# Turning the attention weights by a transposing DMA instead of TensorE, with the start and the end of the attention stage rearranged

## The chip, the cores and the metric

The kernel runs on one core of one Trainium2 chip. The metric is the device time of one execution in microseconds (us); the median of three executions stands below. Everything after that section comes from one profiled execution.

## What is computed

Four layers are applied to `x` (64 sequences of 64 tokens, 512 channels, float32), each added to its input; `c` is a condition vector for each sequence.

```python
def attention(x, c):                       # 16 heads of 32 channels
    scale, shift = split(c @ W_emb + b_emb)
    xn = rms_norm(x, g_norm) * (1 + scale) + shift
    q, k, v = heads(xn @ W_qkv)
    P = softmax(rms_norm(q, g_q) @ rms_norm(k, g_k).T * 32 ** -0.5)
    o = P @ v
    return o + o @ W_out
x = x + attention(x, c)
x = x + sample(x, c)       # each channel becomes w0 * x[i0] + w1 * x[i0 + 1]
x = x + gru(c, x)          # h0 = c; 64 steps with W_ih, W_hh
x = x + oscillators(c, x)  # q0 = p0 = c; 64 steps of Runge-Kutta 4, four tanh(q) @ coupling.T in a step
```

## The kernel before

Each matrix product is made of float16 halves (a high part and a rest, so three products for one), accumulated in float32. A "low" operation computes the rest of a value whose high part has been rounded.

**Stage one** (to about 640 us) does attention and sampling on 32 pairs of sequences, 128 tokens on the 128 partitions. It is a software pipeline written out by hand: slot `i` of each engine holds pieces of five pairs. On TensorE (PE) the order of a slot is: `turn_qk` (q and k of pair i-1), `project(i, 0)`, `scores(i-1)`, `turn_p(i-2)`, `project(i, 1)`, `mix(i-2)` (P @ v), `project(i, 2)`, `proj(i-2)`, `sample(i-3)`, `turn_x(i+2)`. Every engine runs its own list in order and waits on semaphores. After the slots, the last pairs (N3, N2, N1, N0, with N0 the very last) are written out one by one.

The part around the change is the path of P. `scores` leaves the logits in PSUM (`psB`); `least` (VectorE, DVE) takes minima; `exps` (ScalarE, ACT) writes `S`, 16 activations a pair, the last 14 at the end of the slot; `invert_sum` (DVE) and `norm_p` (GpSimd, POOL) normalize `S` (128 x 1024 float32). In the next slot `turn_p` makes eight float32 transposes of 128 x 128 into `psA`, `high_p` (ACT) and `low_p` (DVE) copy them, in two parts, into the float16 halves of `PT`, and `mix` reads `PT`.

Sampling of pair p: the sync engine's queue (SP) loads row numbers (`load_rows`), DVE builds one-hot matrices `E` (`build`), `high_x1` and `low_x1` (ACT, POOL) split the attention result, `move_x1` copies it one row further by three SBUF-to-SBUF transfers (tap 1), `sample` multiplies both taps by `E`, `weigh_taps` (DVE) and `add_taps` (POOL, two operations for a sequence) add the result to `XR`. ACT's line L483 is one helper for all its operations, so its rows are told apart by the tiles.

In the same stage, weights for the second stage are converted piece by piece (`load_wr`, `high_wr`, `low_wr`, `store_wih`), with stage buffers in `room`.

**Stage two** (from about 644 us) is 64 steps of both recurrences. `first()` begins with `high_xs(0)` (ACT), which waits for all taps of all pairs, then `low_xs(0)` (POOL), then on PE `gi_front(0)` and the other gate products of step 0, `stage(0, 0)` (the first coupling product of the oscillators, which needs only the condition), then `gi_front(1)`. There is one buffer `xs`: `high_xs(1)` waits until the gate products of step 0 have read it.

Of the kernel before, what the change touches and what calls it, by code (L numbers as in the profile page):

```python
# [5 lines left out]
ALU = mybir.AluOpType  # L6
# [55 lines left out]
def program(nc, x, cond, W_emb, b_emb, g_norm, W_qkv, g_q, g_k, W_out, W_ih, W_hh, b_ih, b_hh,  # L62
# [9 lines left out]
    with ExitStack() as ctx:  # L72
# [22 lines left out]
        x2_done = sem("x2_done")  # L95
        first4 = sb("first4", [PART, 4, KC, B])
        block = ctx.enter_context(nc.Block())
        with ExitStack() as s:
            attention_and_sampling(nc, ctx, s, block, banks, S, x2_done, first4, XR, condT, ident, Wx, later, x, cond, W_emb, b_emb, g_norm,
                                   W_qkv, g_q, g_k, W_out, W_ih, W_hh, b_ih, b_hh, coupling, bias, rows_dram, wih_dram)  # L100
        with ExitStack() as s:
            recurrences(nc, ctx, s, block, banks, S, x2_done, first4, XR, condT, later, out)


def attention_and_sampling(nc, sems, ctx, block, banks, S_, x2_done, first4, XR, condT, ident, Wx, later, x, cond, W_emb, b_emb, g_norm,
# [37 lines left out]
    split = [front[:, 2 + u, :].bitcast(F16).rearrange("p (i n) -> p i n", i=2) for u in range(2)]  # L143
# [7 lines left out]
    hs0 = first4[:, 0, :, :].rearrange("p c b -> p (c b)").bitcast(F16).rearrange("p (i c b) -> p i c b", i=2, c=KC)  # L151
    S = sb("S", [PART, HEADS, T])
# [12 lines left out]
    stage = [room[k % 2][:, (2 + k // 2) * D:(3 + k // 2) * D] for k in range(4)]  # L165
# [18 lines left out]
    Elast = [room[u][:, KC * D // 2:].bitcast(F16).rearrange("p (c n) -> p c n", c=KC) for u in range(2)]  # L184
    psE = psQ[:, 0, :].rearrange("p (m b) -> p m b", m=2 * KC)
    xT = psB[:, 0, :].rearrange("p (c b t) -> p c b t", c=KC, b=2)
    rsT = psB[:, 1, 0:PART]

# [24 lines left out]
    cond_T, cond_kept, w1_T, emb_done, mod_step = (sem(n) for n in ("cond_T", "cond_kept", "w1_T", "emb_done", "mod_step"))  # L213
    wq_hi, wq_ready, wq_scaled, brz_done = (sem(n) for n in ("wq_hi", "wq_ready", "wq_scaled", "brz_done"))
    wv_hi, wv_ready, mod_ready, wo_scaled, gain_step = (sem(n) for n in ("wv_hi", "wv_ready", "mod_ready", "wo_scaled", "gain_step"))
    x_in = [sem(f"x_in{u}") for u in range(2)]
    rows_in = [sem(f"rows_in{u}") for u in range(2)]
    last_blank, x1_moved, last_moved = sem("last_blank"), sem("x1_moved"), sem("last_moved")
# [16 lines left out]
    wr_in = [sem(f"wr_in{k}") for k in range(4)]  # L235
# [38 lines left out]
    def _(sp):  # L274
# [46 lines left out]
        def slot(pair, i):  # L321
            if p := pair(3):
                load_x(p)
# [13 lines left out]
            if 0 <= i + 2 - WR_FROM < WR_PIECES:  # L337
                load_wr(i + 2 - WR_FROM)
# [8 lines left out]
        for k in range(3 * KC):  # L347
            if k == 0:
                load_x(FIRST2[0])
            if k == 0:  # L350
                for at, g in ((10 * KC, g_q), (10 * KC + 1, g_k)):
                    sp.dma_start(vrows[at:at + 1, :].rearrange("a (q n) -> a q n", n=DH),
                                 g.rearrange("(a q n) -> a q n", a=1, q=1).broadcast_to([1, PART // DH, DH])).then_inc(rows_of_v_in, 16)
# [17 lines left out]
    def _(pool):  # L371
# [30 lines left out]
        def add_taps(p, b):  # L402
            pool.wait_ge(um_done, p.n * 2 + b + 1)
            us = um[b][:, :, 0, :]
            nc.gpsimd.tensor_tensor(us, us, um[b][:, :, 1, :], ALU.add).then_inc(us_done, 1)
            pool.wait_ge(us_done, p.n * 2 + b + 1)
            r = of_b(p, b)
# [31 lines left out]
        def slot(pair, i):  # L439
# [1373 lines left out]
```

## Time and profile before

| | |
|---|---|
| three runs | 1569.5, 1569.72, 1570.03 us; median 1569.72 |
| the profiled execution | 1567.16 us |
| its span (first to last instruction) | 1565.3 us |
| PE busy | 1511.4 us, 97% |
| DVE busy | 1360.1 us, 87% |
| ACT busy | 943.3 us, 60% |
| POOL busy | 688.2 us, 44% |

The span is cut into instructions of each engine, with the time an engine sat idle before one in square brackets and what ended the wait. A "line" is the line of the source. A timeline row merges instructions that follow each other: its first number is when the first began, its second how long they took. PE's own lengths are modelled: a row ends a little after the next one begins, so the time of a group is read from one start to the next.

### The profile page before, as it was taken

The numbers are of one execution on the slowest core, as the hardware profiler recorded it, in microseconds if no ns is written. First come the engines' busy times: TensorE is split into PE (matmuls) and PEld (weight loads), VectorE is DVE, ScalarE is ACT, GpSimd is POOL, SyncE is SP. The second block draws the span as 40 slices with busy tenths as digits, with TensorE's granted clock in tenths as the row PEclk, the third lists the DMA queues.
The fourth block names the chain that finished last, engine by engine and source line by source line (L and its number), as shares of the span: only waits on it lengthen the run. The fifth ranks groups of instructions, "written<-read, shape, count | busy, mean of one in ns | idle before, by whom it ended". The sixth has DMA issues, their size and how long they took to land.

```text
span 1565.3 us, 95993 instructions
## 1 busy us (share of the span) xinstructions
PE 1511.4 (97%) x42395; PEld 1347.4 (86%) x42395; DVE 1360.1 (87%) x3317; ACT 943.3 (60%) x2884; POOL 688.2 (44%) x853
## 2 busy tenths in 40 slices
PE   5999999999999999899999999999999999999994
PEld 3577777777777777899999999999999999999994
DVE  7988888888888888589989899989998999899997
ACT  6677776777777764355555555555555555555553
POOL 2455555555555554434343434334343434334331
PEclk8999999999999999999999999999999999999998
DMA  6112221222222213000000000000000000000001
GB/s 226 40 58 58 63 58 56 62 65 70 73 70 77 63 33 111 23 11 15 13 14 15 15 14 12 16 15 14 13 13 15 15 14 12 15 15 15 13 13 16
DMA packets 106658, 59.87 MB, mean 38 GB/s; under 512 B 77369, under 2 KB 91873, under 8 KB 106241
## 3 DMA queue, kind: packets, MB, share of 16 engines
q1 hardware_dynamic: 106160, 53.71, 13.2%
q8 instruction: 333, 5.46, 1.5%
q14 instruction: 85, 0.69, 0.1%
q10 hardware_dynamic: 80, 0.02, 0.0%
HBM read 33.71 MB, written 11.60 MB: 29 GB/s over the span
## 4 chain that ended last, share of the span: by engine, by line
PE 92%; DVE 3%; issue 2%; ACT 0%; DMA 0%; SPq 0%; POOL 0%; POOLq 0%; DVEq 0%; ACTq 0%
PE psB L1390 34%; PE psA L1419 15%; PE psQ L1108 14%; PE psA L1424 7%; PE psQ L1149 7%; PE psO L1179 5%; PE psO L1167 2%; PE psA L1117 2%; PE psB L1131 2%; PE psA L1086 2%; PE psB L1188 1%; DMA vrows<-in_L_cond_g_k 0%; DVE Wx L837 0%; DVE room L751 0%; PE psQ L1204 0%
## 5 line engine op out<-in xcount | busy, mean ns | idle before, releaser
L1390 PE MATMUL psB<-first,Wx 128*128 128x64 f16 x9216 | 290.9, 193 | 3.3 <-issue 2.4
L1419 PE MATMUL psA<-ts,Cp 128*128 128x64 f16 x8192 | 283.0, 193 | 11.1 <-ACT ts L1458 10.8
L1390 PE MATMUL psB<-first,Whh 128*128 128x64 f16 x9072 | 286.4, 193 | 0.7
L1390 PEld LDWEIGHTS psB<-first,Wx 128*128 128x128 f16 x9216 | 278.2, 98 | 4.2 <-issue 3.9
L1390 PEld LDWEIGHTS psB<-first,Whh 128*128 128x128 f16 x9072 | 273.7, 98 | 1.5 <-issue 1.4
L1108 PE MATMUL psQ<-Wx,front 128*128 128x512 f16 x1152 | 267.4, 382 | 4.6 <-DVE front L914 3.9
L1458 ACT ACTIVATE ts<-qst 128x256 f16<-128x256 f32 x192 | 80.1, 417 | 314.5 <-DVE qst L1561 314.5
L1419 PEld LDWEIGHTS psA<-ts,Cp 128*128 128x128 f16 x8192 | 258.0, 98 | 12.5 <-ACT ts L1458 11.7
L1108 PEld LDWEIGHTS psQ<-Wx,front 128*128 128x128 f16 x1152 | 110.7, 98 | 122.3 <-DVE front L914 4.1
L1424 PE MATMUL psA<-ts,Cp 128*128 128x64 f16 x4096 | 162.4, 193 | 0.0
L1699 POOL TENSOR_TENSOR en<-rz,dn 128x256 f32<-128x256 f32 x64 | 46.7, 729 | 256.6 <-issue 255.8
L1424 PEld LDWEIGHTS psA<-ts,Cp 128*128 128x128 f16 x4096 | 137.9, 98 | 0.0
L412 POOL TENSOR_TENSOR S<-S,rden 128x1024 f32<-128x1024 f32 x32 | 60.9, 1904 | 172.0 <-DVE rden L813 172.0
L1588 DVE TENSOR_TENSOR ts<-psA,ts 128x256 f16<-128x256 f32 x256 | 107.7, 421 | 31.5 <-ACT psA L1458 26.1
L483 ACT ACTIVATE S<-psB,mn 128x64 f32<-128x64 f32 x448 | 132.9, 337 | 1.6 <-DVE mn L797 1.6
L751 DVE TENSOR_SCALAR room<-rows,lidx 128x512 f16<-128x512 f16 x256 | 126.9, 538 | 0.0
L1561 DVE SCALAR_TENSOR_TENSOR rest<-cub,psQ 128x256 f32<-128x256 f32 x256 | 106.6, 416 | 6.9
L1149 PE MATMUL psQ<-x,room 128*128 128x128 f16 x1856 | 108.5, 219 | 0.0
L1561 DVE SCALAR_TENSOR_TENSOR psO<-qst,psO 128x256 f32<-128x256 f32 x256 | 106.6, 416 | 0.0
L1699 POOL TENSOR_TENSOR V<-X3b,first 128x256 f32<-128x256 f32 x64 | 46.8, 731 | 136.0 <-DVE first L1683 135.9
L1149 PEld LDWEIGHTS psQ<-x,room 128*128 128x128 f16 x1856 | 104.9, 98 | 0.1
L483 ACT ACTIVATION_READ_ACCUMULATOR S<-psB,mn 128x1 f32 x448 | 103.5, 231 | 0.0
(192 smaller groups left out, 3021.6 us busy)
## 6 DMA issues: line engine op xcount, KB each, us to landing
front<-in_x SPq DMA_DIRECT2D x32, 256.0 KB, 2.6
rows<-rows_dram SPq DMA_DIRECT2D x64, 128.0 KB, 2.9
out<-ot SPq DMA_DIRECT2D x512, 16.0 KB, 1.8
x<-x SPq DMA_DIRECT2D x29, 224.0 KB
Whh<-in_L_cond_W_qkv SPq DMA_DIRECT2D x12, 256.0 KB, 6.7
room<-in_L_cond_W_hh SPq DMA_DIRECT2D x12, 256.0 KB, 3.0
room<-in_L_cond_W_ih SPq DMA_DIRECT2D x12, 256.0 KB, 2.8
wih_dram<-front SPq DMA_DIRECT2D x12, 256.0 KB, 3.0
```

The lines of the kernel that those rows point to most:

```text
L483: return nc.scalar.activation(out, in_, f, **k)
L751: e = v.tensor_scalar(E_of(p, b)[:, k, :], rows[b][:, :], lidx[:, k:k + 1], None, ALU.is_equal)
L1108: last = mm(psQ[:, n, :], xn[p.u][:, i, c, :], Wqkv[:, j, c, n * D:(n + 1) * D], start=(c == 0 and t == 0), stop=(c == KC - 1 and t == 2))
L1149: last = mm(o[:, m, :, :], E_of(p, b)[:, c, m * PART:(m + 1) * PART], x1_of(p)[:, :, i, c, b, :], start=(c == 0 and i == 0), stop=(c == KC ...
L1179: last = mm(psO[:, m, :], Wo[:, i, c, m * PART:(m + 1) * PART], oT[:, j, c, :], start=(c == 0 and t == 0), stop=(c == KC - 1 and t == 2))
L1390: last = mm(o, W_[:, i, c, g * PART:(g + 1) * PART], src[:, j, c, :], start=False, stop=False, skip_group_check=True)
L1419: mm(psF[:, s % 2, m, :], Cp[:, i, c, m * PART:(m + 1) * PART], ts_[:, 0, c, :], start=(c == 0 and m == 0 and i == 0), stop=False, skip_gr ...
L1424: last = mm(psF[:, s % 2, m, :], Cp[:, 0, c, m * PART:(m + 1) * PART], ts_[:, 1, c, :], start=False, stop=(c == KC - 1), skip_group_check= ...
L1458: return nc.scalar.activation(out, in_, f, **k)
L1561: return v.scalar_tensor_tensor(out=flat(out), in0=flat(in0), scalar=scalar, in1=flat(in1), op0=ALU.mult, op1=op1)
L1588: v.tensor_tensor(ts_[:, 1, :, :], th, ts_[:, 0, :, :], ALU.subtract).then_inc(S["ts_ready"], 1)
L1699: return nc.gpsimd.tensor_tensor(flat(out), flat(in0), flat(in1), op)
```

## The change

For pairs 0 to 29 (N2) P is no longer turned by PE. ACT's `high_halves` and POOL's `low_halves` split `S` as it lies (128 x 1024) into `halves`, and SP's `turn_p` sends one transposing DMA of 128 x 2048 float16 (512 KB) from `halves` into `PT`. `mix` waits for that transfer. N1 and N0 are still turned by PE. To make room, `load_wr` has two stage buffers, not four, and `split` lies in `room`.

At the start, `g_q` and `g_k` are loaded from ACT's queue and not SP's; `low_wq` of two pieces stands ahead of the slots, and `grid_middle` (two casts on DVE) in slot 1 and not ahead of slot 0; `modulation` stands behind `newton` and one `low_wq`.

At the end, the last pair is sampled in two parts: tap 0 (which needs no moved copy) and then tap 1; `weigh_last_taps` and `first_taps` do the first two time steps on their own, so that `high_xs(0)` waits only for these. The oscillators' first coupling product stands in stage one behind the last sample.

```diff
@@ sync engine
+        def turn_p(p):
+            sp.wait_ge(pl_done, p.n + 1)
+            need(sp, mix_done, p.n)
+            sp.dma_start_transpose(PT[:, :, :, :].rearrange("p i j n -> p (i j) n"), halves.rearrange("p i s k -> p (i s k)"))\
+                .then_inc(pt_in, 16)
...
         def slot(pair, i):
+            if p := pair(-2):
+                turn_p(p)
             if p := pair(3):
                 load_x(p)
...
-            if k == 0:
-                for at, g in ((10 * KC, g_q), (10 * KC + 1, g_k)):
-                    sp.dma_start(vrows[at:at + 1, :].rearrange("a (q n) -> a q n", n=DH),
@@ GpSimd
+        def first_taps(p, b):
+            pool.wait_ge(um_first, b + 1)
+            us = um[b][:, :, 0, 0:FIRST_T]
+            nc.gpsimd.tensor_tensor(us, us, um[b][:, :, 1, 0:FIRST_T], ALU.add).then_inc(us_first, 1)
+            pool.wait_ge(us_first, b + 1)
+            r = of_b(p, b)[:, :, 0:FIRST_T]
+            nc.gpsimd.tensor_tensor(r, r, us, ALU.add).then_inc(x2_first, 1)
...
+        def low_halves(p):
+            pool.wait_ge(ph_done, p.n + 1)
+            nc.gpsimd.tensor_tensor(halves[:, 1, :, :], S[:, :, :], halves[:, 0, :, :], ALU.subtract).then_inc(pl_done, 1)
...
             if p := pair(-1):
                 norm_p(p)
+                if p.n <= N2.n:
+                    low_halves(p)
@@ ScalarE
+        def high_halves(p):
+            act.wait_ge(p_done, p.n + 1)
+            need(act, pt_in, p.n * 16)
+            a(halves[:, 0, :, :], S[:, :, :]).then_inc(ph_done, 1)
...
-            if p := pair(-2):
-                high_p(p, 0)
-                high_p(p, 1)
...
             if 0 <= i - WR_FROM < WR_PIECES:
                 high_wr(i - WR_FROM)
+            if p := pair(-1):
+                high_halves(p)
...
-        high_p(N2, 1)
-        high_v(N0)
         high_o(N2)
         high_qk(N0, 0)
         high_qk(N0, 1)
+        high_v(N0)
...
         high_o(N0)
+        a(Q0, condT[:, :, :]).then_inc(S_["Q_done"], 1)
+        act.wait_ge(S_["Q_done"], 1)
+        a(ts_[:, 0, :, :], Q0, ACT.Tanh).then_inc(S_["ts_hi"], 1)
+        a(th0, Q0, ACT.Tanh).then_inc(S_["th_done"], 1)
         high_x1(N0)
@@ VectorE
-            if p := pair(-2):
-                low_p(p, 0)
-                low_p(p, 1)
...
+        for k in range(2 * KC + 2, 3 * KC):
+            low_wq(k)
-        grid_middle()
...
-        build(N1, 1, (0, 1, 2))
+        build(N1, 1, range(KC))
         residual(N0)
-        build(N1, 1, (3,))
...
-        weigh_taps(N0, 0)
-        weigh_taps(N0, 1)
+        dve.wait_ge(S_["th_done"], 1)
+        v.tensor_tensor(ts_[:, 1, :, :], th0, ts_[:, 0, :, :], ALU.subtract).then_inc(S_["ts_ready"], 1)
+        weigh_last_taps(0)
+        weigh_last_taps(1)
@@ TensorE
             if b == 0:
-                pe.wait_ge(pt_ready, p.n + 1)
+                if p.n <= N2.n:
+                    pe.wait_ge(pt_in, 16 * (p.n + 1))
+                else:
+                    pe.wait_ge(pt_ready, p.n - N2.n)
...
-            if p := pair(-2):
-                turn_p(p)
...
-        sample(N0, 0)
-        sample(N0, 1)
+        sample_last(0, 0)
         cell_from_condition(2)
+        sample_last(1, 0)
+        sample_last(0, 1)
+        sample_last(1, 1)
+        oscillators_from_condition()
@@ stage two
             if n == 0:
+                act.wait_ge(x2_done, B - 2)
+                act.wait_ge(x2_first, 2)
+            if n == 2:
                 act.wait_ge(x2_done, B)
...
-            stage(Pair(0, 0, 0), 0)
             gi_front(1)
```

PE, one middle slot before, from `turn_qk` to `sample`:

```order
L1086 MATMUL psA<-ident,qn 128x128 x8
L1108 MATMUL psQ<-Wx,front 128x512 x12
L1131 MATMUL psB<-first 64x64 x96
L1117 MATMUL psA<-ident,S 128x128 x8
L1108 MATMUL psQ<-Wx,front 128x512 x12
L1167 MATMUL psO<-PT,Vt 32x64 x96
L1108 MATMUL psQ<-Wx,front 128x512 x12
L1179 MATMUL psO<-oT,Wo 128x128 x48
L1149 MATMUL psQ<-x,room 128x128 x64
```

and the same slot after:

```order
L1141 MATMUL psA<-ident,qn 128x128 x8
L1163 MATMUL psQ<-Wx,front 128x512 x12
L1187 MATMUL psB<-first 64x64 x96
L1163 MATMUL psQ<-Wx,front 128x512 x12
L1241 MATMUL psO<-PT,Vt 32x64 x96
L1163 MATMUL psQ<-Wx,front 128x512 x12
L1253 MATMUL psO<-oT,Wo 128x128 x48
L1205 MATMUL psQ<-x,room 128x128 x64
```

The row `psA<-ident,S` is gone; in the new slot `mix` (`psO<-PT,Vt`) follows `project(i, 1)` as before, with eight transposes less ahead of it.

POOL, the end of one middle slot and the next, after:

```order
L432 TENSOR_TENSOR S<-S,rden 128x1024
L437 TENSOR_TENSOR front<-S,front 128x1024
L453 TENSOR_TENSOR front<-front,modA 128x512
L453 TENSOR_TENSOR front<-front,modB 128x512
L425 TENSOR_TENSOR um<-um 128x4x64
L428 TENSOR_TENSOR XR<-XR,um 128x4x64
L425 TENSOR_TENSOR um<-um 128x4x64
L428 TENSOR_TENSOR XR<-XR,um 128x4x64
L447 TENSOR_TENSOR x<-XR,x 128x4x64 x2
L460 TENSOR_TENSOR front<-front 128x512
```

The row `front<-S` is `low_halves` (`halves` lies in the tensor `front`). It stands between `norm_p` and the next slot's `modulate` (`modA`, `modB`), ahead of the adding of taps (`um`) and of `low_x1` (`x<-XR,x`); before the change nothing stood there.

SP, one middle slot after:

```order
L317 DMA_TRANSPOSE PT<-front 128x16x128
L285 DMA front<-in_x 128x512
L289 DMA rows<-rows_dram 128x512
L302 DMA x<-x 112x1024
L302 DMA x<-x 15x1024
L304 DMA x<-x 1x2x384
L312 DMA room<-in_L_cond_W_ih 128x512
L323 DMA wih_dram<-room 256x1x512
L289 DMA rows<-rows_dram 128x512
```

The transposing DMA is the first row of the slot; all others are as before and wait behind it.

PE, the last pair and the first step of the recurrences, before:

```order
L1149 MATMUL psQ<-front,room 128x128 x64
L1225 MATMUL psB<-first,Whh 128x64 x48
L1149 MATMUL psQ<-qn,room 128x128 x64
L1225 MATMUL psB<-first,Whh 128x64 x48
L1380 UNCONDITIONAL_BRANCH
L1390 MATMUL psB<-first,Wx 128x64 x144
L1419 MATMUL psA<-ts,Cp 128x64 x32
L1424 MATMUL psA<-ts,Cp 128x64 x16
L1390 MATMUL psB<-first,Wx 128x64 x144
```

and after:

```order
L1205 MATMUL psQ<-front,room 128x128 x64
L1299 MATMUL psB<-first,Whh 128x64 x48
L1219 MATMUL psQ<-qn,room 128x64 x32
L1299 MATMUL psB<-first,Whh 128x64 x48
L1219 MATMUL psQ<-qn,room 128x64 x96
L1308 MATMUL psA<-ts,Cp 128x64 x48
L1462 UNCONDITIONAL_BRANCH
L1472 MATMUL psB<-first,Wx 128x64 x288
L1472 MATMUL psB<-first,Whh 128x64 x144
```

The sample of N0 (`psQ<-qn,room`) is in two parts, with the last gate products from the condition (`first,Whh`) between; the coupling product (`psA<-ts,Cp`) has moved from between the gate products of steps 0 and 1 (`psB<-first,Wx`, 144 each) to ahead of both.

## Rows read from the trace of the kernel before

**Rows 1.** Windows: length, busy PE, PEld, DVE, ACT, POOL; clock, DMA share, GB/s.

```profile
66.00:586.80 520.80, 517.02 (x10077) 380.72 (x10074) 445.27 (x845) 376.43 (x1422) 279.76 (x278) 1.00 0.21 62
```

**Rows 2.** Timeline of PE, one slot: start us, us, engine, line, operation, count.

```profile
310.90 1.04 PE L1086 MATMUL psA<-ident,qn 128*128 128x128 f32 x8
...
315.36 1.09 PE L1117 MATMUL psA<-ident,S 128*128 128x128 f32 x8
...
316.29 2.75 PE L1108 MATMUL psQ<-Wx,front 128*128 128x512 f16 x12
...
318.97 1.20 PE L1167 MATMUL psO<-PT,Vt 64*32 64x64 f16 x96
...
325.38 3.74 PE L1149 MATMUL psQ<-x,room 128*128 128x128 f16 x64
...
329.51 1.04 PE L1086 MATMUL psA<-ident,qn 128*128 128x128 f32 x8
```

**Rows 3.** Source line L1190, the last transpose of a slot.

```profile
L1190 PE MATMUL psB<-ident,rs x32: 272/273/323, 17.3 to 571.3; 128*128 128x128 f32 x32
```

**Rows 4.** Timeline of DVE, ACT and POOL in the same slot.

```profile
317.12 1.29 DVE L790 TENSOR_TENSOR PT<-psA,PT 128x512 f16<-128x512 f32 x2
...
319.08 0.60 ACT L483 ACTIVATE front<-psQ 128x512 f32<-128x512 f32 x1 [0.99 <-PE psQ L1108]
...
325.40 0.25 DVE L813 RECIPROCAL rden<-den 128x16 f32<-128x16 f32 x1 [1.16 <-ACT S L483]
...
325.73 1.90 POOL L412 TENSOR_TENSOR S<-S,rden 128x1024 f32<-128x1024 f32 x1 [5.07 <-DVE rden L813]
...
312.18 1.09 POOL L429 TENSOR_TENSOR front<-front,modA 128x512 f32<-128x512 f32 x1 [3.02 <-DVE front L738]
...
317.93 1.61 POOL L423 TENSOR_TENSOR x<-XR,x 128x256 f16<-128x256 f32 x2
```

**Rows 5.** Groups by form, POOL, 82 to 585; timeline, ACT.

```profile
L436 POOL TENSOR_TENSOR front<-front 128x512 f16<-128x512 f32 x27 | 31.4, 1164 | 0.0
...
604.47 1.06 ACT L483 ACTIVATE S<-S 128x1024 f32<-128x1024 f32 x1 [0.81 <-DVE S L802]
```

**Rows 6.** Source L318 (512 KB loads); page, part 6; queues, 700 to 1500.

```profile
DMA to landing us min/median/max: 4.2/5.8/8.4
...
out<-ot SPq DMA_DIRECT2D x512, 16.0 KB, 1.8
...
q1 hardware_dynamic: 65154, 7.44, 6.4%
```

**Rows 7.** Timeline of the start.

```profile
11.57 0.33 PE L1270 MATMUL psO<-ident,vrows 42*128 42x42 f32 x1 [2.79 <-DMA vrows<-in_L_cond_g_k]
...
12.38 2.35 DVE L842 SCALAR_TENSOR_TENSOR room<-Wo,room 128x1024 f16<-128x1024 f32 x2
...
25.57 1.38 DVE L866 CAST x<-um 64x512 int32<-64x512 f32 x1
...
39.14 0.75 DVE L730 SCALAR_TENSOR_TENSOR first<-psA,gqk,first 128x512 f16<-128x512 f32 x1 [1.59 <-ACT first L483]
```

**Rows 8.** Timeline of the last pairs and of the first recurrence step.

```profile
601.49 0.60 ACT L483 ACTIVATE Vt<-psQ 128x512 f16<-128x512 f32 x1 [2.20 <-PE psO L1167]
...
633.06 1.47 SPq L294 DMA_DIRECT2D qn<-qn  x2
...
635.39 2.31 DVE L751 TENSOR_SCALAR room<-rows,lidx 128x512 f16<-128x512 f16 x4
...
637.22 3.73 PE L1149 MATMUL psQ<-qn,room 128*128 128x128 f16 x64 [2.55 <-issue]
...
643.49 0.42 ACT L1458 ACTIVATE first<-XR 128x256 f16<-128x256 f32 x1 [9.33 <-POOL XR L408]
...
644.76 4.54 PE L1390 MATMUL psB<-first,Wx 128*128 128x64 f16 x144 [2.41 <-issue]
...
649.34 0.42 ACT L1458 ACTIVATE first<-XR 128x256 f16<-128x256 f32 x1 [0.35 <-PE psB L1390]
```

More of the change, by code:

```diff
@@ L142, in attention_and_sampling @@
     rsB = sb("rsB", [PART, PART])
-    split = [front[:, 2 + u, :].bitcast(F16).rearrange("p (i n) -> p i n", i=2) for u in range(2)]
+    halves = front[:, 2:4, :].rearrange("p v n -> p (v n)").bitcast(F16).rearrange("p (i s k) -> p i s k", i=2, k=T)
     xa = front[:, 4, :].rearrange("p (c b t) -> p c b t", c=KC, b=2)
@@ L164, in attention_and_sampling @@
     wo32, cp32 = (r.rearrange("p (c n) -> p c n", c=KC) for r in room)
-    stage = [room[k % 2][:, (2 + k // 2) * D:(3 + k // 2) * D] for k in range(4)]
+    stage, split32 = ([room[v][:, (2 + k) * D:(3 + k) * D] for k in range(2)] for v in range(2))
+    split = [a.bitcast(F16).rearrange("p (i n) -> p i n", i=2) for a in split32]
     x1_last = [a.rearrange("p v n -> p (v n)").bitcast(F16).rearrange("p (v i c b t) -> p v i c b t", v=2, i=2, c=KC, b=2)
@@ L184, in attention_and_sampling @@
     Elast = [room[u][:, KC * D // 2:].bitcast(F16).rearrange("p (c n) -> p c n", c=KC) for u in range(2)]
+    psF0, th0 = (psA[:, n, 0:KC * B].rearrange("p (c b) -> p c b", c=KC) for n in range(2))
     psE = psQ[:, 0, :].rearrange("p (m b) -> p m b", m=2 * KC)
@@ L187, in attention_and_sampling @@
     rsT = psB[:, 1, 0:PART]
+    FIRST_T = 2
     def x1_of(p):
@@ L745, in build @@
                     need(dve, samp_done, p.n * 2 + b - 1)
+                elif b == 1:
+                    for u in range(2):
+                        dve.wait_ge(wih_out[u], 3 * KC // 2 * 16)
                 if p.n == 0:
@@ L1082, in turn_qk @@
             pe.wait_ge(qn_done, p.n * 2 + 2)
-            need(pe, pt_ready, p.n - 1)
+            need(pe, qk_ready, p.n)
+            if p.n == 0:
+                pe.wait_ge(cond_kept, 1)
             for n in range(2):
@@ L1151, in sample, with sample_last @@
             last.then_inc(samp_done, 1)
+        def sample_last(b, tap):
+            if tap:
+                pe.wait_ge(last_moved, 96)
+            else:
+                pe.wait_ge(x1_ready, NP)
+                pe.wait_ge(e_built, N0.n * 2 + b + 1)
+                pe.wait_ge(um_done, N0.n * 2 + b - 1)
+            for m in range(KC):
+                for c in range(KC):
+                    for i in range(2):
+                        last = mm(psL[b][:, m, tap, :], E_of(N0, b)[:, c, m * PART:(m + 1) * PART], x1_of(N0)[:, tap, i, c, b, :],
+                                  start=(c == 0 and i == 0), stop=(c == KC - 1 and i == 1))
+            if tap:
+                last.then_inc(samp_done, 1)
         def mix(p, b):
@@ L1227, in cell_from_condition, with oscillators_from_condition @@
                 last.then_inc(S_["gn_done"], 1)
+        def oscillators_from_condition():
+            for i, j in TERMS:
+                pe.wait_ge(S_["ts_ready"] if j else S_["ts_hi"], 1)
+                for c in range(KC):
+                    for m in range(KC):
+                        last = mm(psF0[:, m, :], Cp[:, i, c, m * PART:(m + 1) * PART], ts_[:, j, c, :],
+                                  start=(c == 0 and m == 0 and (i, j) == (0, 0)), stop=(c == KC - 1 and i == 1), skip_group_check=True)
+            last.then_inc(S_["f_done"], 1)
         def slot(pair, i):
```

152 lines of the change are left out of this document (83 added, 69 removed).

## The prediction

> **What bounds the kernel now.** I read the windows first, stage by stage. In slots 3 to 29 PE is busy 517.0 of 520.8 us (99.3%) at the full granted clock, level 2.4 GHz; DVE has 86%, ACT 72%, POOL 54% [rows 1]. So these slots cost what PE's list costs, and another engine matters only where it makes PE wait. The timeline of PE gives one slot: from `turn_qk` at 310.90 to the next at 329.51 is 18.61 us; the eight transposes of P take from 315.36 to 316.29, 0.93 us; `mix` begins at 318.97, 8.07 us into the slot; `sample` at 325.38 [rows 2]. The last transpose of a slot runs 32 times, the last at 571.3 [rows 3]. The reader should see two things there: no gap between PE's groups, and the place of `mix`, because that is where the new path ends. Outside these slots PE waits: at the start on loads and on DVE's conversions, at the end on chains through all engines and a DMA [rows 7, 8].
>
> **Middle slots: what goes.** PE loses 0.93 us a slot. For PE-bound slots that is the gain, if nothing new is waited for: slots 3 to 30 and the tail's transposes of N2, 29 times, 27.0 us. DVE also loses its two copies (1.29 us [rows 4]) and ACT its own; neither is the bound, so I count nothing.
>
> **Middle slots: the new chain.** Its end must come before `mix`. From rows 4: `norm_p` starts at 325.73 and takes 1.90, so P is ready at 327.63, 1.88 us before the next slot begins. All of this follows PE's `project(i, 1)` (ACT's square of it is at 319.08), which itself comes 0.93 earlier, so the distance to the next slot stays 1.88. Then `high_halves`: 1024 columns on ACT from SBUF to SBUF, as the exponential of S, 1.06 us [rows 5]; at that place ACT is idle, its row of `Vt` and one weight piece being done by about 326.4. `low_halves` on POOL: between the 1.90 of `norm_p`, with the same columns, and twice the 1.164 of a 512-column difference to f16, 2.33 [rows 4, 5]. With 0.05 between steps the transfer can be issued 1.2 to 1.6 us into the next slot; I take 1.3. `mix` comes 8.07 - 0.93 = 7.14 us into it. So the transfer has 5.8 us from issue to landing (5.5 to 5.9). The SP queue before it is empty then, and what it delays (the load of x three pairs ahead, a row load) is not used in this slot.
>
> The trace has no transposing DMA. Bounds for 512 KB: below, plain loads of 512 KB land in 4.2 us at best, 5.8 in the middle, several queued at a time [rows 6]. Above: if the turned side is written in pieces of 32 bytes, 16384 of them, at the price that the small packets of the output have (6.4% of 16 engines over 800 us for 65154 packets is 12.6 ns of one engine each), that is 16384 x 12.6 / 16 ns = 12.9 us, plus the 1.8 us that a 16 KB transfer takes: 14.7 [rows 6]. If only its rows of 256 bytes count, 2048 packets, the sum is 1.6 + 1.8 = 3.4. I take 5.0: same bytes as the plain load, alone in its queue, and nothing in the trace that makes the turned side slow; this is the weakest number here. At 5.0 it lands at 6.3, 0.8 ahead of `mix`, and costs PE nothing.
>
> The general rule for landing time L: from the start of `mix` to the next issue the chain is 18.61 + 1.3 - 8.07 = 11.85 us long (`mix`, the copy of its result, 14 exponentials, sum, norm, halves), and mix waits for L. The period is the larger of 17.68 and 11.9 + L. L = 5.8 is free, L = 6.7 eats the whole 0.93, and beyond it each us costs about 29.
>
> Here the Trainium skill speaks both ways. "VectorE: DVE Perf Modes", The three transpose paths, gives 1309 ns for one 128 x 128 block by the crossbar DMA; sixteen in a row would be an estimated 21 us, and the sum would be more than 400 us slower. "Advanced Engine Details and Errata", X-Bar Transpose (TRN2), expects 350 to 400 GB/s, an estimated 1.4 us of data for 512 KB, and the sum stays as below. No row here decides between them.
>
> **POOL.** It gains 1.9 to 2.3 us a slot, in front of `modulate`, which starts 1.28 into the slot now [rows 4]: a delay of 0 to 0.35. Behind it stand adding taps and `low_x1`, ending at 319.54, back to back; then `move_x1`, whose data in the tail are awaited from 633.06 to 637.22, 4.2 us [rows 8]. Copied to this slot: 319.54 + 4.2 = 323.7, and `sample` starts at 325.38 - 0.93 = 324.45. The margin falls from 1.6 to 0.7, or 0.4 with the delay. I count 0; if the cover goes, each 0.1 us is 3 us in all.
>
> **Start.** PE's transpose of the vectors waits 2.79 us for `g_k` until 11.57; behind it are 72 products of the embedding, and DVE's next weight halves (12.38, 2.35 long) [rows 7]. From ACT's queue `g_k` comes earlier; then those two halves set the end: the last cannot start before about 11.5 and ends near 12.7, so modulation comes about 2.4 earlier, less some tenths since ACT issues two more DMAs. The casts (1.38 for the first [rows 7]) leave a place where all waits for DVE, for two weight halves that cost as much, and go to a slot where DVE waits 1.59 at 39.14. Together I take -2.5 (0 to -4).
>
> **Tail.** (a) `high_o(N2)` no longer stands behind `high_v(N0)` (0.5 us from 601.49): -0.5. (b) `residual(N0)` stands behind one more one-hot piece: +0.35. (c) The last sample starts at 637.22, when its moved copy is there. One would expect that half the sample before this saves half; but tap 0 of the second sequence needs `E`, built from 635.39 to 637.70 [rows 8]. So after 637.70 PE does three quarters of the sample, 3 x 1.04 at 32.5 ns a product: it ends at 640.8, as now (640.95). What is gained is behind it: `high_xs(0)` at 643.49 and the gates at 644.76. With two time steps, weighing and two additions of 8 columns are about 0.8 us in all; ACT's 0.42 and POOL's 0.67 follow; gates at about 642.8: -2.0. (d) The oscillators' product, 1.4 us of PE, goes ahead into this wait. But the gates of step 1 need `xs(1)`, which ACT starts at 649.34, when those of step 0 are read; its 0.42, POOL's 0.7 and the waits fill the 1.3 us that the product fills today. So -0.1, not -1.4. The 62-column remainders of the additions lie beside PE's 4.5 us of gates [rows 8].
>
> **Sum.** -27.0 - 2.5 - 0.5 + 0.35 - 2.0 - 0.1 = -31.75 on the profiled execution of 1567.16 us: 1535.4. The median of runs is 2.56 above it: 1538.
>
> **Rivals.**
> - The transfer lands late by part of a us (L between 5.9 and 6.6). For it: loads of the same size have 5.8 in the middle. Against: those were queued. At L = 6.3 a slot loses 0.5, in all 14: 1552.
> - The transfer is slower than the gain, the other side: L above 6.9 with the 4.7 us of the ends counted. Place: PE's first product of `mix`, waiting for the DMA in each slot. At L = 8.5 the period is 20.4, 1.8 more than now, x 29 = 52, less 4.7: about 1617. At 14.7: period 26.6, 1796. For it: every turned element is scattered, and the path has never run here. The page's 1309 ns is this case too.
> - POOL becomes what PE waits for: `low_x1` late by 1 us through slower operations beside DVE. `sample` then waits 0.6 a slot, 17 in all: 1555. Against: POOL at 54% plus 1.9 us of 17.7 is under 70%.
> - The change does not do what it says because the transposes were hidden: PE has no gap there, so I give it 0.02, and it would be the ends alone, 1565.
>
> **How the numbers follow.** My forecast 0.56, with its own range 1533 to 1546 (the start 0 to -4, POOL's margin, a few tenths a slot); late by a part 0.13; POOL 0.07; slower than the gain 0.20; nothing in the slots 0.02; the rest, 0.02, near the start. Within 0.2% (3.1 us), which is what a measurement of this kernel can tell, lies only a narrow band of L around 6.8: 0.02. Faster 0.77, slower 0.21. The range reaches from 1532 over both partial cases to 1566 and leaves out the slow case.
>
> **What would show it.** Right: slots of about 17.7 us, no wait of PE at `mix`, the DMA landing in 5.8 us or less, start of stage two some 29 us plus 2.4 earlier, `sample` without waits. Wrong first if PE's `mix` waits for `PT` from the DMA: then the period minus 11.9 is L. Wrong in the margin if PE waits at `sample` for the moved copy. The start is right if PE's vector transpose no longer waits 2.8 us, the tail if gates follow the last sample by about 2 us and not 3.8.

## The result and the profile after

Six runs of the changed kernel have a median of 1560.76 us (1557.17 to 1563.98), six of the kernel before beside them 1570.84 (1569.5 to 1574.44). The ratio is 0.9939, with an interval of 0.992 to 0.9959: a gain of 0.6%, about 10 us, clear of the noise. Forecast were 32 us less than the kernel before. Two later measurements of the same kernel gave 0.9941 and 0.9948. On one chip the kernel before ran 6 to 9 us faster than on the others, so from here on ratios are compared, not times.

The profiled execution took 1563.98 us (span 1562.2) against 1567.16 (1565.3) before; it is the slowest of its six. The windows of the slots, columns as in [rows 1]:

```profile
66.00:586.80 520.80, 504.04 (x10009) 361.04 (x10007) 458.73 (x798) 379.93 (x1400) 343.88 (x312) 1.00 0.40 91
```

PE is busy 96.8% of it and was 99.3%: it waits now, at the full clock. The timeline of PE, the first product group of some slots (start, length):

```profile
46.93 1.09 PE L1141 MATMUL psA<-ident,qn 128*128 128x128 f32 x8 [0.29 <-DVE qn L824]
...
107.45 0.82 PE L1141 MATMUL psA<-ident,qn 128*128 128x128 f32 x6
...
143.53 0.71 PE L1141 MATMUL psA<-ident,qn 128*128 128x128 f32 x5
...
325.02 1.04 PE L1141 MATMUL psA<-ident,qn 128*128 128x128 f32 x8
...
342.71 0.49 PE L1141 MATMUL psA<-ident,qn 128*128 128x128 f32 x3
...
563.49 0.71 PE L1141 MATMUL psA<-ident,qn 128*128 128x128 f32 x5
...
581.09 1.04 PE L1141 MATMUL psA<-ident,qn 128*128 128x128 f32 x8
```

and the same in the kernel before:

```profile
50.03 0.66 PE L1086 MATMUL psA<-ident,qn 128*128 128x128 f32 x4 [0.28 <-DVE qn L780]
...
106.16 0.60 PE L1086 MATMUL psA<-ident,qn 128*128 128x128 f32 x4
...
143.38 0.82 PE L1086 MATMUL psA<-ident,qn 128*128 128x128 f32 x6
...
571.42 0.82 PE L1086 MATMUL psA<-ident,qn 128*128 128x128 f32 x6
```

Read three things. The slot at 325.02 is 17.69 us long, which is 18.61 less the whole 0.93. The 23 slots from 143.53 to 563.49 have a mean of 18.26, though, against 18.61 before: 0.35 won, not 0.93. They mostly alternate: 17.7 to 18.1, then 18.2 to 19.1 (the one at 342.71 takes 19.11). And the start is 3.10 us ahead at 46.93, yet at 107.45 the kernel is 1.29 us behind.

What PE waits for in those stretches (60 to 575: us in total, times, longest), and how long a transfer takes:

```profile
PE psO L1241 <- DMA PT<-front: 5.4, 6, 1.6
PE psB L1187 <- DVE first L774: 2.9, 2, 1.7
PE psQ L1163 <- issue: 2.1, 2, 1.1
PE psO L1241 <- issue: 1.9, 6, 0.6
PE psO L1253 <- DVE oT L881: 1.2, 4, 0.4
```

```profile
L317 SPq DMA_TRANSPOSE PT<-front x30: 1364/1904/2937, 53.6 to 583.1; - x30
...
DMA to landing us min/median/max: 4.3/4.7/6.1
```

The waits for P are not the whole loss. Read from group start to group start, the 23 slots take 12.9 us more than 17.69 each: 6.8 in `project(i, 1)` and ahead of `mix` (3.8 of them waits for P, 2.1 two pauses), 2.9 inside `mix` (1.5 of them pauses), 1.6 ahead of `proj`, whose `oT` comes late from DVE, and 1.4 around `scores`, whose `low_qk` is DVE's too. A pause is idle time in the middle of a group, the rows with "issue", for which the profile shows nothing that was waited for; the kernel before has none in these slots.

The last pairs and the first recurrence step, as [rows 8]:

```profile
632.52 0.42 ACT L1539 ACTIVATE first<-XR 128x256 f16<-128x256 f32 x1 [9.78 <-POOL XR L420]
...
633.79 4.36 PE L1472 MATMUL psB<-first,Wx 128*128 128x64 f16 x144 [0.75 <-issue]
...
636.90 0.42 POOL L1826 COPY first<-condT 128x256 f32<-128x256 f32 x1
...
637.35 0.51 ACT L1539 ACTIVATE Zp<-first,alphas 128x256 f32<-128x256 f32 x1 [4.14 <-POOL first L1826]
...
638.25 1.28 ACT L1539 ACT_TABLE_LOAD   x1
...
640.71 0.40 ACT L1539 ACTIVATE first<-XR 128x256 f16<-128x256 f32 x1
...
641.91 6.97 PE L1472 MATMUL psB<-first,Wx 128*128 128x64 f16 x144 [3.76 <-POOL first L1784]
...
655.19 1.10 PE L1501 MATMUL psA<-ts,Cp 128*128 128x64 f16 x32
```

The gates of step 0 begin 10.97 us sooner than in [rows 8]. The stage at 655.19 began at 661.24 before: 6.05 sooner, so step 0 gives 4.92 back: 2.32 because the gates of step 1 follow those of step 0 by 8.12 us and not 5.80, 2.60 because they take longer. Its copy of P now follows the four rows of 62-column additions on GpSimd; `of_p`, the table load, sigmoids, a seed and `high_xs(1)` follow on ScalarE, and then come 6.97 us of products that took 4.36 a step earlier.

### The profile page after: what moved, and what is told of

It is laid out like the page before. It is cut to its first block, busy times and chain, and to the rows that moved or that the text cites. A ratio compares the mean times of both kernels' runs of the same rounds, so it can differ in the third digit from the quotient of the medians.

```text
span 1562.2 us, 95585 instructions
## 1 busy us (share of the span) xinstructions
PE 1497.6 (96%) x42219; PEld 1327.1 (85%) x42219; DVE 1363.3 (87%) x3259; ACT 942.4 (60%) x2854; POOL 750.1 (48%) x887
## 4 chain that ended last, share of the span: by engine, by line
PE 82%; DVE 5%; ACT 4%; issue 3%; POOL 3%; DMA 2%; ACTq 0%; POOLq 0%; DVEq 0%
PE psB L1472 34%; PE psA L1501 15%; PE psQ L1163 10%; PE psA L1506 7%; PE psQ L1205 6%; PE psO L1253 4%; DMA PT<-front 2%; ACT S L515 2%; PE psO L1241 2%; PE psB L1187 1%; PE psA L1141 1%; POOL S L432 1%; POOL front L437 1%; ACT front L515 1%; DVE room L795 1%
## 5 line engine op out<-in xcount | busy, mean ns | idle before, releaser
L795 DVE TENSOR_SCALAR room<-rows,lidx 128x512 f16<-128x512 f16 x256 | 158.0, 659 | 0.2 <-issue 0.2
```

What stands on the lines that cost most here:

```text
L795: e = v.tensor_scalar(E_of(p, b)[:, k, :], rows[b][:, :], lidx[:, k:k + 1], None, ALU.is_equal)
```

## What held the slots

The cause is three engines away from PE. The slot at 325.02 (short itself; what is late in it makes the next one long), timeline of POOL, DVE and ACT:

```profile
333.46 1.16 POOL L460 TENSOR_TENSOR front<-front 128x512 f16<-128x512 f32 x1
...
333.70 0.95 DVE L804 TENSOR_SCALAR ms<-ss 128x33 f32<-128x33 f32 x1
334.57 0.60 DVE L795 TENSOR_SCALAR room<-rows,lidx 128x512 f16<-128x512 f16 x2
334.69 0.23 ACT L515 ACTIVATE lm<-ms 128x33 f32<-128x33 f32 x1 [0.64 <-DVE ms L804]
```

and the kernel before, the same place of a slot (POOL, then DVE):

```profile
319.49 1.17 POOL L436 TENSOR_TENSOR front<-front 128x512 f16<-128x512 f32 x1
...
320.50 0.20 DVE L760 TENSOR_SCALAR ms<-ss 128x33 f32<-128x33 f32 x1
```

`means` is a step of 33 columns. Before, it came at the very end of POOL's `low_x` in every second slot and behind it in the others, and took 0.18 to 0.25. Now PE's list is 0.93 shorter and POOL's is not, so `means` meets `low_x` or `low_x1`, and ends when that one ends: 334.65 against 334.62. The groups by form (66 to 586.8: count, busy, mean ns) say that this is no single case, first before, then after:

```profile
L760 DVE TENSOR_SCALAR ms<-ss 128x33 f32<-128x33 f32 x27 | 5.1, 188 | 3.2 <-DVE ss L773 0.5
```

```profile
L795 DVE TENSOR_SCALAR room<-rows,lidx 128x512 f16<-128x512 f16 x228 | 143.4, 669 | 0.2 <-issue 0.2
L804 DVE TENSOR_SCALAR ms<-ss 128x33 f32<-128x33 f32 x27 | 19.4, 719 | 2.9
L515 ACT ACTIVATE lm<-ms 128x33 f32<-128x33 f32 x27 | 6.2, 230 | 8.7 <-DVE ms L804 8.5
```

Behind `lm` on ACT stand the 14 exponentials of the other pair, then `rden`, `norm_p`, the halves and the DMA, issued at +1.3 us of one slot and +2.2 of the next. The late halves push POOL's run later in turn, and the next `means` meets another part of it; hence the alternation. That was **T1**; that the runs of POOL and DVE shift each other in this way is argued from the rows, not tried. **T2**: the transfer itself (median 4.7 us) is what is late. **T3**: VectorE is full (the builds of E, L795, went from 533 to 669 ns). The Trainium skill has a rule in SBUF — State Buffer, Who interferes with whom: VectorE in a two-port mode, which a `tensor_scalar` can enter, contends with GpSimd, and whichever issues second fully blocks for the whole instruction; a VectorE instruction with two SBUF inputs contends with a GpSimd one that reads SBUF; a `tensor_reduce` never contends on trn2. The rows agree: 0.95 for `means` beside `low_x`, and the reduction ahead of it kept its 0.69 beside `low_x1`. Which mode `means` ran in, no row shows.

## The experiments

Ratios are to the kernel before on the same chip. "Slots" is the mean of the same 23 slots; "step 0" is the time from the gates of step 0 to the first stage of step 1.

| run | ratio | interval | slots | step 0 |
|---|---|---|---|---|
| kernel before | 1 | | 18.61 | 16.48 |
| changed (the result) | 0.9939 | 0.992 to 0.9959 | 18.26 | 21.40 |
| `e0_changed_again` | 0.9941 | 0.9922 to 0.996 | 18.16 | 21.08 |
| `e16_changed_third` | 0.9948 | 0.9934 to 0.9961 | 18.25 | 21.09 |
| `e1_ends_alone` | 0.9978 | 0.9964 to 0.9992 | 18.61 | 20.35 |
| `e2_means_other_form` | 0.9947 | 0.9928 to 0.9966 | 18.15 | 20.05 |
| `e4_early_p_copy` | 0.9931 | 0.9909 to 0.9953 | 18.15 | 16.30 |
| `e5_two_transfers` | 0.9926 | 0.9904 to 0.9948 | 18.10 | 20.35 |
| `e7_guess_from_sums` | 0.9886 | 0.9865 to 0.9907 | 17.89 | 21.42 |
| `e8_guess_two_transfers` | 0.9871 | 0.9851 to 0.9892 | 17.81 | 18.81 |
| `e9_all` (e8, e4) | 0.984 | 0.982 to 0.9861 | 17.78 | 16.30 |
| `e10_head_first` | 0.9942 | 0.9929 to 0.9954 | 18.19 | 20.36 |
| `e11_four_edits` (e9, e10) | 0.9843 | 0.983 to 0.9857 | 17.73 | 16.30 |
| `e12_load_x_later` | 0.9941 | 0.9929 to 0.9954 | 18.11 | 20.28 |
| `e13_before_guess` | 0.9986 | 0.9977 to 0.9995 | 18.61 | 16.31 |
| `e14_first_two_by_pe` | 0.9813 | 0.9798 to 0.9828 | 17.78 | 16.38 |
| `e15_first_three_by_pe` | 0.9802 | 0.9782 to 0.9822 | 17.81 | 16.30 |

**The ends alone.** All pairs turned by TensorE, as in the kernel before; the rest of the change stays.

> The changed kernel with P turned by TensorE for every pair, so that only the rearranged start and end differ from the kernel before. Theory A (the trace of the changed kernel, first step of the recurrences): the ends win 0.9 us at the start and 2.2 us at the gates of step 0, and the first recurrence step gives 4.9 us back, because ScalarE's of_p, its table load and its sigmoids stand behind the copy of P on GpSimd and the clock then falls: ratio 1.000 to 1.002, 1570 to 1573 us. Rival B (the prediction's own terms, nothing given back): -2.5 at the start, -2.4 in the tail: ratio 0.997, about 1566 us. Gates of step 1 at 641 to 643 less 8.4 of slots, that is +8.4: near 650, and 7 us long by A, 4.4 us long and starting 1 to 2 us after the gates of step 0 end by B.

Measured 0.9978, about -3 us. In the profile the slots of 66 and 104 us begin 2.3 us sooner than before (64.74, 103.90), the gates of step 0 4.04 us (640.72), and step 0 takes 20.35 us. So both hold in part: the terms of start and tail are there as B had them, and the give-back is there as A had it (+3.9 us). The two nearly cancel in this profile (the first stage of step 1 at 661.07 us against 661.24), so where the 3 us of the timed runs come from, it does not show.

**Means in another form.**

```
-v.tensor_scalar(ms[:, cols], ss[:, cols], 1.0 / DH, EPS * WS * WS, ALU.mult, ALU.add)
+v.scalar_tensor_tensor(out=ms[:, cols], in0=ss[:, cols], scalar=1.0 / DH,
+                       in1=epsK[:, 0:1].broadcast_to(...), op0=ALU.mult, op1=ALU.add)
```

> The changed kernel with VectorE's step `means` (128x33) as a scalar_tensor_tensor, with the constant read from a [128,1] tile, rather than a tensor_scalar. Theory T1 (that instruction runs into GpSimd's long stretch of low_x1 and low_x and only ends with it, 744 ns against 186 before; guess, exps, rden, norm_p, the halves and the transfer stand behind it): means takes 0.15 to 0.4 us, the transposing DMA is issued at +1.3 us of every slot, the middle slots come to 17.7 to 17.9 us rather than 18.26, and the time to 1548 to 1554 us (ratio 0.986 to 0.989). Rival T2 (the transfer itself is too slow, 4.3 to 6.1 us from issue to landing): nothing but the 0.05 to 0.1 us that means was on ScalarE's way; slots 18.1 to 18.3, ratio 0.992 to 0.995. Rival T3 (VectorE is full, since build, sums and means are all slower in the shorter slot): means stays at 0.5 us or more, or the wait moves to the next VectorE step, scale_qk or build; ratio 0.992 to 0.995.

Nothing came of it, 0.9947, slots 18.15:

```profile
L808 DVE SCALAR_TENSOR_TENSOR ms<-ss,epsK 128x33 f32<-128x33 f32 x27 | 20.1, 746 | 2.8
```

T1's numbers missed, and as written T3 took this run. But each `means` beside POOL's run still ended 0.04 to 0.07 us after one of POOL's instructions, as in the changed kernel (0.03 to 0.05). The new form has two SBUF inputs, the other case of the rule above, so this run did not take the meeting with POOL away and decides nothing between T1 and T3. The step had to be moved instead:

**Guess from the sums.** ACT takes the logarithm of the sums itself; `means` moves behind `low_o`, where POOL is idle. So two things wait no longer behind a late `means`: ACT's exponentials, and DVE's own `low_o`.

```
-            act.wait_ge(ms_done, k + 1)
-            a(lm[:, cols], ms[:, cols], ACT.Ln)
+            act.wait_ge(ssq_done, qk.n * 2 + 2)
+            a(lm[:, cols], ss[:, cols], ACT.Ln, scale=1.0 / DH, bias=eps[:, 0:1])
```

> The changed kernel with ScalarE taking its logarithm straight from the sums of squares (scale and bias in the activation) in the 30 guesses of the pairs, so that it no longer waits for VectorE's means, which moves behind low_o, ahead of newton. The run before it (means in another form) left means ending 0.03 to 0.06 us after an instruction of GpSimd in every slot, so the form was no test of T1. T1 (ScalarE's guess and 14 exps wait for a VectorE instruction that ends only with GpSimd's low_x1 or low_x, and so the transfer is issued late in every other slot): idle of ScalarE ahead of lm falls from 10 us in all to under 2, the transfer is issued at +0.8 to +1.4 in every slot, slots 17.7 to 17.9 us against 18.2, time -8 to -11 us: ratio 0.986 to 0.989. T3 (VectorE's builds of E, stretched beside the same GpSimd run, make low_o late, and proj waits for it): means goes, the wait of 0.4 to 0.7 us for oT stays in the long slots or comes into all of them, slots 18.0 to 18.3: ratio 0.991 to 0.994. T2 (the transfer takes 6 us at times): the few waits of 1 us for PT stay, 0.2 us a slot in the mean.

0.9886, slots 17.89, as T1 has it:

```profile
L517 ACT ACTIVATE lm<-ss,eps 128x33 f32<-128x33 f32 x27 | 8.5, 315 | 0.0
L810 DVE TENSOR_SCALAR ms<-ss 128x33 f32<-128x33 f32 x27 | 4.5, 167 | 0.0
```

ACT no longer waits there, the DMA is issued at +1.56 to +1.58 in each of the 13 slots that begin from 196 to 411 us (T1 had +0.8 to +1.4), and 11 of the 23 slots take 17.69 to 17.70. PE's waits for `oT` are gone and one wait for P of 0.5 us is left. T3 falls as it was written: the builds became slower still (702 ns) and it cost nothing. What is left is 4.3 us over 17.69 a slot, 3.7 of them inside `mix`, where the profile shows PE pausing (107 to 545 us):

```profile
PE psO L1247 <- issue: 2.3, 6, 0.5
```

**The control**, the same edit in the kernel before:

> Control: the kernel before with ScalarE's logarithm taken straight from the sums, the edit that brought the changed kernel from ratio 0.9941 to 0.9886. T1 says that the wait for means exists only where the means meet GpSimd's run of low_x1 and low_x, as they do in the changed kernel; in the kernel before means take 0.18 us behind that run and nothing waits long: ratio 0.998 to 1.001, slots 18.61 us. Rival T4 (the edit is a gain by itself, whatever the transfer does): ratio 0.993 to 0.996, slots below 18.5 us.

The slots stay at 18.61 to the hundredth. The ratio of 0.9986 is a small gain, and it lies in the first slots (1.74 us by 67 us). The edit is worth its 0.3 us a slot only where the changed kernel made `means` meet POOL. The two runs together show that cause. They don't share the cost out between ACT's late exponentials and DVE's late `low_o`, since the edit frees both.

**Two transfers.** The high half is sent while POOL makes the low one.

```
+            for i, done in enumerate((ph_done, pl_done)):
+                sp.wait_ge(done, p.n + 1)
+                sp.dma_start_transpose(PT[:, i, :, :], halves[:, i, :, :]...).then_inc(pt_in, 16)
```

> The changed kernel with the transposing DMA in two of half the size: the high half issued once ScalarE has written it, the low half behind GpSimd's low_halves. Theory T2 (the transfer's 512 KB at 217 GB/s are what is late): only 256 KB are left to move behind low_halves, the second lands 1.0 to 1.5 us sooner, mix never waits for it, slots 17.7 to 17.9 us, ratio 0.986 to 0.989. T1 (the issue is late by 0.9 us in every other slot) expects the same here, since 2.2 + 3.2 lies under 5.8: this run prices the transfer and does not part T1 from T2. Rival: the landing time is mostly fixed (issue 1.9 us on the queue for each, 2 us of latency), so that the second lands no sooner or later than the one did, and load_x and the other loads stand behind 1.9 us more of issuing: slots 18.3 to 18.8, ratio 0.994 to 1.002.

> The run above and the transfer in two parts (high half ahead of low_halves) together. T1 with the rest of T2: slots 17.69 us in nearly all, no wait for PT from 80 us on, ratio 0.985 to 0.988, 1 to 4 us below the run above. T3: as the two transfers alone, slots alternating 17.7 and 18.4, ratio 0.992 to 0.994.

Alone 0.9926, slots 18.10, almost strictly 17.69 and 18.4 in turn; with the guess 0.9871, slots 17.81. In the first, PE no longer waits for P in the 23 slots (3.8 us in the changed kernel), but 3.0 us for `oT`, 8 times. T2 and T1 had both expected 17.7 to 17.9 here, so both missed: with P in time, DVE's late low half holds PE instead. The transfer's size is a second cause of at most 0.1 us a slot; that is as much as the changed kernel's own repetitions differ by (18.16 to 18.26), and the intervals of both pairs of runs overlap. The other load of T2, that of x issued right behind, was held back:

> The changed kernel with the load of x three pairs ahead held on the SP queue until the transposing DMA of the slot has landed, so that nothing of the kernel's own is under way beside it. Theory L1 (the landings of 5.6 to 6.1 us, 7 or 8 of 29, against 4.3 to 4.8 for the others, come from sharing the DMA engines with that load): every landing 4.3 to 4.8 us, TensorE waits for PT 0 to 1 us in all rather than 5.4, time -2 to -4 us, ratio 0.991 to 0.993. Rival L2 (they come from something else, such as the instruction fetches, one of which lies in the transfer each time): 5 to 8 landings over 5.5 us again, ratio 0.993 to 0.996, or slower by what the later load of x and of the rows costs.

L2 holds: 0.9941, no change, and landings up to 5.9 us still, 4 of 29 from 71 us on above 5.5. The changed kernel had 8, its repetition 6, and `e7_guess_from_sums`, with the load in its old place, 2, so 4 is no sign of an effect:

```profile
DMA to landing us min/median/max: 4.3/4.6/5.9
```

Why some land 1.3 us late is open.

**The first step of the recurrences.**

```
+        pool.wait_ge(um_done, N0.n * 2 + 2)
+        nc.gpsimd.tensor_copy(first4[:, 3, :, :]..., condT[:, :, :]...).then_inc(S_["P_done"], 1)
         add_taps(N0, 0, FIRST_T)      # the 62-column additions
...
-            nc.gpsimd.tensor_copy(flat(P), flat(condT)).then_inc(S["P_done"], 1)
```

> The changed kernel with the copy of P for the first recurrence step issued on GpSimd behind the low half of the input of step 0 and ahead of the additions of 62 columns, not behind them. Theory G1 (ScalarE's of_p, table load 1.28 us, sigmoids 0.6, seed 0.6, high_xs(1) 0.4 and GpSimd's low_xs(1) 0.67 follow one another behind that copy, and the wait lets the clock fall): of_p at about 635, high_xs(1) at 638.3 to 638.6 rather than 640.71, gates of step 1 at 639.3 to 639.8 rather than 641.91, and 4.4 rather than 6.97 us long: -2.1 to -4.7 us, ratio 0.991 to 0.992. Rival G2 (the clock falls for another reason): the gates start 2.1 us earlier, still 7 us long: -2.1, ratio 0.9925. Rival G3 (the recurrences have slack after step 0): no change, 0.994.

The steps are G1's; its ratio (0.991 to 0.992) the run missed. The gates of step 1 in the timeline of PE:

```profile
636.21 4.37 PE L1474 MATMUL psB<-first,Wx 128*128 128x64 f16 x144 [1.26 <-POOL first L1786]
```

They follow those of step 0 (630.59) by 5.62 us, not 8.12, and take 4.37, not 6.97: step 0 is 16.30 us against 21.40. The timed ratio of this run alone, 0.9931, does not tell 5 us from nothing; with the other edits it does:

> The run above (guess from the sums, two transfers) with the early copy of P as well. The early copy took the first stage of the recurrences from 21.4 to 16.3 us behind the gates of step 0, which the other runs had at 20.1 to 20.4. If the three add up: 4 to 5 us below the run above, ratio 0.982 to 0.985 (1540 to 1545 us). If the recurrences give it back, as they differ by 3 to 4 us from run to run already, the ratio is that of the run above within 0.001.

0.984 against 0.9871 without it, and each of its five runs (1541.29 to 1544.53 us) is below each of the six without (1545.76 to 1552.19) on the same chip.

**The first slots.** At 107.45 us the changed kernel was 4.39 us worse than its start. The timeline of ACT there:

```profile
68.18 1.06 ACT L515 ACTIVATE front<-S 128x1024 f16<-128x1024 f32 x1 [4.55 <-POOL S L432]
69.15 0.26 ACT L515 ACTIVATE rsB<-psB 128x128 f32<-128x128 f32 x1
69.30 0.68 ACT L515 ACTIVATE first<-psA,gqk 128x512 f16<-128x512 f32 x1
```

P is normalised late for the first two pairs, whose sum is VectorE's work; `high_halves` waits for it, and the next slot's `keep_rs` and `high_qk` stand behind it, which PE's scores need.

> The changed kernel with keep_rs and high_qk of the slots that begin at 46.9 and 66.2 us issued on ScalarE ahead of high_halves of the slot before, not behind it. Theory H1 (in these early slots P is normalised late, high_halves waits 2.3 and 4.6 us for it, and behind it on ScalarE stand rsB and high_qk, for which VectorE's low_qk and TensorE's scores wait 2.6 and 1.6 us): scores without a wait of more than 0.4 us in both slots, the slot at 66.2 begins 1 to 2.5 us sooner, the one at 107.4 2 to 4 us sooner, ratio 0.991 to 0.993. Rival H2 (mix sets the end there, since the halves are as late as before and the transfer lands at 77.2): scores come sooner and mix waits for PT that much longer; the slot at 107.4 within 0.7 us of where it is, ratio 0.993 to 0.996.

H2 holds. The slot at 107.45 comes 0.65 us sooner, and other waits take the place. With all four edits there were 21.91 us in the slot at 65.62 still, and four builds of E in it took this long, beside POOL's `low_halves` and modulation:

```profile
69.26 5.17 DVE L811 TENSOR_SCALAR room<-rows,lidx 128x512 f16<-128x512 f16 x4
```

(Before, 2.05 for the same four at 70.61; in the changed kernel 3.03, in a slot as long, 21.78.)

> The four edits together: guess from the sums, two transfers, the early copy of P, and keep_rs and high_qk ahead of high_halves in the two early slots. If H1 holds, 2 to 3 us below the run with the first three (1543.8 us, ratio 0.984): ratio 0.981 to 0.983, about 1541. If H2 holds, 0.983 to 0.985. The prediction's 1538 us stands 31 to 33 us below the kernel before, ratio 0.979 to 0.980.

0.9843: no better than e9_all. Whether the slower builds cost time here, as T3 has it, is not shown: 3.03 and 5.17 us of them stand in slots of the same length. The first pairs went back to TensorE:

> The first three edits (guess from the sums, two transfers, early copy of P) with the first two pairs turned by TensorE as in the kernel before, so that pairs 2 to 29 go by DMA. Theory J1 (in the first slots P is normalised late, since subtract_least and sum_p are VectorE's there, and the DMA path then has ScalarE's queue, GpSimd's low_halves beside the four builds, and the transfer all late): slots at 66 and 87 us as with TensorE for all (19.95 and 19.2 us), the slot at 105 begins at 102 to 104.5 us rather than 105.9 to 107.4, the middle slots stay at 17.7 to 17.9 us; 1.5 to 3.5 us below the first three edits: ratio 0.981 to 0.983. Rival J2 (the loss comes with the first DMA pair, whichever it is): the slots at 87 and 105 us take the 2 to 4 us instead, ratio 0.984 to 0.986.

> The same with three pairs by TensorE. J1: within 1 us of the run beside it: it pays 0.93 us more of TensorE's transposes and saves what pair 2 still loses in the slot at 87 us. J2: again 2 to 4 us lost, one slot later; no better than the first three edits alone (0.984).

J1: 0.9813 and 0.9802, the best versions here, 1.9 and 2.0% below the kernel before, which is what was forecast for the change (0.980); they have three further edits, so that doesn't bear the forecast out. The slot that began at 107.45 begins at 102.47 and 101.88. What these two show is that the loss comes from sending the first pairs by DMA; which of J1's reasons it is, they do not tell. With two pairs the slot at 82.48 still takes 19.99 us (J1 had 19.2), 1.9 of them more than usual ahead of the scores; with three it takes 19.38, and the ratios don't tell the two apart. The third measurement of the changed kernel was the base beside them:

> The changed kernel once more on the same chip as these two: ratio 0.993 to 0.996, slot at 107 us beginning at 106.5 to 108 us.

0.9948, the slot at 107.52.

## Why the prediction was wrong in size

The direction was right, and the 10 us are a third of what was forecast. The profiled executions differ by these terms (of the 29 times 0.93 us, the prediction counted slots 3 to 30 and the tail's transposes of N2, so two of the first three slots):

| term | forecast | measured |
|---|---|---|
| start, up to 46.93 | -2.5 | -3.10 |
| first three slots, to 107.45 | -1.9 | +4.39 |
| 26 slots, to 581.09 | -24.2 | -9.68 |
| N2's transposes, `high_o`, residual, first taps: gates of step 0 | -3.1 | -2.58 |
| step 0 | -0.1 | +4.92 |
| the other recurrence steps | 0 | +2.95 |

The last term is no steady effect of the change: from the first stage of step 1 to the end the kernel before took 904.1 us, the changed one 907.0 in this execution and 902.7 and 902.8 in two others.

**The step that failed first** is this sentence of the part on the middle slots: "All of this follows PE's `project(i, 1)` (ACT's square of it is at 319.08), which itself comes 0.93 earlier, so the distance to the next slot stays 1.88." Between the square and `norm_p` stands `means` on DVE, and what it met was POOL's list, which did not come earlier. In the slot at 325.02 `norm_p` starts 14.68 us behind `turn_qk`, where 13.90 were forecast and 14.83 was the time before. The trace had the warning: in the kernel before `means` starts (320.50) 0.16 us before `low_x` ends. Moving it brought 0.27 to 0.37 of the missing 0.58 us a slot. Of the rest, the pauses of PE are the larger part: 3.7 us of the 4.3 left in `e7_guess_from_sums`, 0.16 a slot. They were in no row of the kernel before, and their cause is open.

**The rule for L was right** and its value nearly: `mix` waits for P only where issue and landing together pass the 7.14 us into the slot. The slot at 454.05 has 1.68 + 6.1 = 7.8, and 0.6 of waiting; those with the issue at +1.3 to +1.6 and a landing under 5.5 have no such wait. What moved was the issue, to +2.2 in every second slot, and it took landings of 5.6 us and more to make that cost anything. So the rival of the late transfer (0.13) came true in part, by 3.8 us in the 23 slots. I took 5.0 for L; measured are 4.3, 4.7, 6.1. As to the Trainium skill's VectorE: DVE Perf Modes, from whose 1309 ns for one block 21 us were worked out in the prediction, that estimate did not hold: 16 blocks in one transfer landed in 4.7 us. A transfer of a single block no run has. The 350 to 400 GB/s of the other estimate were not reached either (200 to 225).

**The place of the price.** "At that place ACT is idle", the prediction's price of nothing for `high_halves`, was true of a middle slot and was carried to all 29. In the first ones ACT waits 2.3 and 4.6 us in `high_halves`, with two steps that PE needs behind it, and POOL's new run lies beside four builds. Those three slots cost 6.3 us against the forecast, and turning three pairs by PE again took 3.9 us off the kernel with the first three edits (that slot at 101.88, not 105.79). POOL's margin at `sample`, the rival that I gave 0.07, never showed: PE has no wait at `sample` in the slots.

**The tail's last term.** "fill the 1.3 us that the product fills today" took the gates of step 1 as hanging on ACT's read of step 0's gates. They hung on the copy of P, which is POOL's and stood behind the additions that I had put "beside PE's 4.5 us of gates" at no cost. Beside them they are; ahead of something that is waited for they are too. The other ends were forecast well: -3.10 for -2.5, and -2.58 for -3.1, of which N2's transposes are 0.9. In the run with the ends alone they were -2.3 by the slot at 66 us and -1.7 in the tail, for -2.15.

## What to carry over

When one engine's list gets shorter, the lists of the others shift against it. A gain worked out on the engine that bounds is only kept if each short VectorE step on the path is looked up against GpSimd's list at its new time; an end that is met within 0.2 us is a warning. A price of nothing holds for the slots in which the cover was seen: look at the first and last ones apart, and name what is queued behind every new waiting instruction. An addition that may be late by itself must not stand ahead of a copy that may not.

## What the chip showed beyond that

- A VectorE instruction of 33 columns took up to 1.22 us beside GpSimd as a `tensor_scalar` and up to 1.09 as a `scalar_tensor_tensor`, against 0.17 to 0.20 alone. ACT's instruction of the same 33 columns took 0.23 in both kernels.
- The transposing DMA moved its 512 KB at 200 to 225 GB/s while its packets were under way (2,112 of the 2,370 between 272.15 and 280.15 us had under 512 bytes), and SyncE was 1.4 to 2.9 us in issuing one.
- After the wait of 3.76 us the clock was at 0.50 (the lower level, 1.2 GHz) from 642 to 647 us of the changed kernel, and at 1.00 again from 648:

```profile
642.00:643.00 1.00, 1.00 (x21) 1.00 (x22) 0.17 (x1) 0.00 (x0) 0.73 (x1) 0.50 0.08 16
...
648.00:650.00 2.00, 2.00 (x76) 2.00 (x72) 0.00 (x0) 0.42 (x1) 0.59 (x1) 1.00 0.04 8
```

  The same wait of 3.7 to 3.8 us was followed by products of 5.6 to 7.0 us in nine of ten profiled executions and by 4.37 in one (e8_guess_two_transfers); a wait of 1.26 us by 4.37 in all five that had it. So the length of the wait alone does not settle it.
- With a transposing DMA in each slot, PE pauses in the middle of a group of matmuls, with nothing to wait for in the profile: in the kernel with the guess from the sums in two neighbouring slots every 89 us or so (from 177, 267, 356 and 445 us), 0.2 to 0.7 us each; in the changed kernel twice for 1 us in `project(i, 1)` (the slots at 342.71 and 434.98) and four times in `mix`. The kernel before has none in its slots. The cause was not tried.
